# The shared expert's loads: a semaphore for each matrix, issued between the parts of the output weights

## The reference

```python
x = x + attn(layernorm(x), w_qkv, w_out, decay)     # linear attention with a decay
x = x + moe(layernorm(x), gate_w, w_gate, w_up, w_down, sw_gate, sw_up, sw_down)
# attn: q, k, v = x @ w_qkv; q, k = elu(q) + 1, elu(k) + 1
#       running_kv, running_k = scans over the tokens with decay sigmoid(decay) per head
#       out = (q * running_kv / clip(sum(q * running_k), 1e-6)) @ w_out
# moe:  8 experts of width 352, the best 2 of each token, weighed with their softmax scores
#       shared = (silu(x @ sw_gate) * (x @ sw_up)) @ sw_down, sw_gate and sw_up 512 x 704,
#       sw_down 704 x 512; out = routed + shared
```

## Time and profile before

| | |
|---|---|
| median of 3 runs | 714.49 us (713.29 to 715.1) |
| the profiled execution | 715.02 us, its span 713.2 us |
| mean granted TensorE clock | 0.972 |
| busy: PE, DVE, ACT, POOL | 663.0, 426.6, 257.1, 231.0 us |
| moved by DMA | 86.89 MB, 122 GB/s on the mean |

### The profile page before, as it was taken

One profiled execution on the slowest core, in us unless ns is written; L12 is line 12 of the kernel. 1 busy time (PEld: TensorE's weight loads), 2 busy tenths in 40 slices (PEclk: granted clock), 3 DMA queues, 4 the chain that ended last, 5 costly groups with the idle time before them and its releaser, 6 DMA issues.

```text
span 713.2 us, 11766 instructions
## 1 busy us (share of the span) xinstructions
PE 663.0 (93%) x3797; PEld 432.7 (61%) x3798; DVE 426.6 (60%) x746; ACT 257.1 (36%) x397; POOL 231.0 (32%) x269
## 2 busy tenths in 40 slices
PE   7868999899989989899999899999999999999992
PEld 6646677578657465556565465665656565656561
DVE  7757996997987753677787777633333333333331
ACT  5336263354342343546665665421111111111110
POOL 6201121322101313334343254124444444444431
PEclk9999999989989899999999999999999999999997
DMA  6561003513422497897564433268777777777753
GB/s 222 174 231 31 16 16 88 160 48 89 107 71 74 109 256 156 213 229 183 146 171 121 95 46 67 47 117 132 132 132 132 132 132 132 132 135 132 133 89 42
DMA packets 111236, 86.89 MB, mean 122 GB/s; under 512 B 79280, under 2 KB 86448, under 8 KB 111200
## 3 DMA queue, kind: packets, MB, share of 16 engines
q1 hardware_dynamic: 88848, 43.94, 25.7%
q0 software_dynamic: 12272, 27.34, 22.6%
q10 hardware_dynamic: 10080, 15.14, 6.8%
HBM read 44.45 MB, written 23.33 MB: 95 GB/s over the span
## 4 chain that ended last, share of the span: by engine, by line
PE 69%; DVE 8%; issue 2%; ACT 2%; DMA 1%; POOL 1%; ACTq 1%; SPq 0%; POOLq 0%; DVEq 0%
PE ps_y L514 17%; PE ps_g L514 16%; PE ps_u L514 15%; PE ring L389 14%; PE turn_h L534 3%; DVE routed L1409 1%; ACTq L373 1%; PE ps_norm L401 1%; DMA out_dram<-y_job,job_tok 1%; PE ps_den L450 1%; PE ring L476 0%; DMA xg_odd<-xn_hl 0%; DVE den L1304 0%; ACT xn L1040 0%; POOL squares L952 0%
## 5 line engine op out<-in xcount | busy, mean ns | idle before, releaser
L1349 DVE TENSOR_TENSOR hidT<-turn_h,hidT 128x384 f16<-128x384 f32 x71 | 39.5, 556 | 112.0 <-ACT hidT L1096 109.8
L945 POOL DMA_INDIRECT out_dram<-y_job,job_tok x39 | 61.9, 1586 | 109.1 <-DVE y_job L1683 102.2
L1092 ACT ACTIVATE silu<-ps_g,job_silu 128x352 f32<-128x352 f32 x39 | 21.6, 553 | 189.5 <-PE ps_g L514 158.9
L389 PE MATMUL ring<-xnT_h,wq_h 128*128 128x512 f32 x192 | 82.0, 427 | 7.5 <-DVE wq_l L1248 2.5
L514 PE MATMUL ps_y<-routed,hidT 128*128 x351 | 82.1, 379 | 1.3 <-DVE hidT L1349 1.3
L855 POOL TENSOR_SCALAR var_eps<-mean_var 128x1 f32<-128x1 f32 x32 | 12.9, 402 | 203.4 <-DVE mean_var L1339 114.9
L389 PE MATMUL ring<-xnT_l,wq_h 128*128 128x512 f32 x192 | 78.6, 410 | 0.0
L389 PE MATMUL ring<-xnT_h,wq_l 128*128 128x512 f32 x192 | 78.3, 408 | 0.0
L514 PE MATMUL ps_g<-routed,x_in 128*128 x468 | 76.4, 313 | 0.0
L514 PE MATMUL ps_u<-routed,x_in 128*128 x468 | 76.2, 313 | 0.0
L952 POOL TENSOR_TENSOR squares<-squares 128x704 bf16<-128x704 bf16 (+1 forms) x24 | 42.3, 1761 | 93.1 <-ACT squares L1060 93.1
(11 more groups left out here) (232 smaller groups left out, 1108.7 us busy)
## 6 DMA issues: line engine op xcount, KB each, us to landing
routed<-in_L_ffn_w_gate_dram ACTq DMA_DIRECT2D x7, 704.0 KB, 4.8
routed<-in_L_ffn_w_up_dram ACTq DMA_DIRECT2D x7, 704.0 KB, 7.7
x_res<-in_L_attn_x_dram SPq DMA_DIRECT2D x18, 256.0 KB, 3.2
out_dram<-x SPq DMA_DIRECT2D x16, 256.0 KB, 3.3
xn_scratch<-xn_hl SPq DMA_DIRECT2D x16, 256.0 KB, 2.4
out_dram<-y_job POOLq DMA_DIRECT2D x16, 256.0 KB, 4.2
x_in<-in_L_attn_x_dram SPq DMA_DIRECT2D x14, 256.0 KB, 2.7
routed<-in_L_ffn_w_down_dram ACTq DMA_DIRECT2D x7, 512.0 KB, 8.9
```

Of the source, the lines that this page charges most:

```text
L389: ins = pe.matmul(ps, a, b, start=(i == 0), stop=(i == len(steps) - 1))
L945: pool.indirect_dma_start(out[:, :], bass.IndirectOffsetOnAxis(job_tok[:, r:r + 1], 0), y_job[:, b, :], None, compute_op=ALU.add).then_inc ...
L1092: act.activation(silu[:, :], ps_g[:, 0:F], ACT.Silu, scale=by).then_inc(s["silu_s"], 1)
L1349: dve.tensor_tensor(hidT[:, 1], turn_h[:, 0:FC, :], hidT[:, 0], ALU.subtract).then_inc(s["hidT_s"], 1)
```

## The change

`shared_in` is replaced by `shared_g`, `shared_u` and `shared_d`, one for gate, up and down. Where SP before issued parts 13, 14, 15, waited for `over_0` and then issued the six shared loads, it now issues gate, part 13, up, part 14, waits for `over_0`, issues the four loads of down and then part 15. Before each square of the shared expert ACT waits for the semaphore of that piece's matrix, where before it waited for all six loads ahead of the first square.

```diff
-            gw_h_s ... cst_a cst_b shared_in
+            gw_h_s ... cst_a cst_b shared_g shared_u shared_d
...
-        SHARED_DMAS = 2 + 2 * HALVES
+        DOWN_DMAS = 2 * HALVES
...
             load_x(TPB)
             load_x(TPB + 1)
-            loads = [(shared[:, GAP + HALVES * at:GAP + HALVES * (at + GU)].rearrange("p (k f) -> p k f", f=HALVES * F),
-                      src.rearrange("(k p) f -> p k f", p=P)) for at, src in ((GATE_AT, sw_gate), (UP_AT, sw_up))]
+
+            def load_shared(at, src, done):
+                sp.dma_start(shared[:, GAP + HALVES * at:GAP + HALVES * (at + GU)]
+                             .rearrange("p (k f) -> p k f", f=HALVES * F),
+                             src.rearrange("(k p) f -> p k f", p=P)).then_inc(s[done], 16)
+
+            def load_shared_down(h):
+                for dst, src in down_parts(shared_raw[HALVES * 2 + h], sw_down[h * F:(h + 1) * F, :]):
+                    sp.dma_start(dst, src).then_inc(s["shared_d"], 16)
+
+
+            load_shared(GATE_AT, sw_gate, "shared_g")
+            load_part(QKV_PARTS + 1)
+            load_shared(UP_AT, sw_up, "shared_u")
+            load_part(QKV_PARTS + 2)
+            sp.wait_ge(s["over_0"], 1)
             for h in range(HALVES):
-                loads += down_parts(shared_raw[HALVES * 2 + h], sw_down[h * F:(h + 1) * F, :])
-            for m in range(QKV_PARTS + 1, PARTS):
-                load_part(m)
-            sp.wait_ge(s["over_0"], 1)
-            for dst, src in loads:
-                sp.dma_start(dst, src).then_inc(s["shared_in"], 16)
+                load_shared_down(h)
+            load_part(QKV_PARTS + 3)
...
                 x, kind, h, w, done = pieces[m]
+                if m < SHARED_PIECES:
+                    act.wait_ge(*((s["shared_g"], 16), (s["shared_u"], 16), (s["shared_d"], 16 * DOWN_DMAS))[kind])
                 if m == 0:
-                    act.wait_ge(s["shared_in"], 16 * SHARED_DMAS)
                     act.wait_ge(s["over_0"], 1)
```

More of the change, by code:

```diff
@@ L249, in preln_decay_attention_moe @@
             al_s out_mm xr0 xr1 x2_s stat2 var2 veps2 rstd2_s shift2_s norm2_s hi2_s xn2_s xg0 xg1 gw_sq_s gw_mm gw_set
-            gw_h_s gw_l_s gate_mm logit_s x2_out0 x2_out1 xn2_out0 xn2_out1 pad_out cst_a cst_b shared_in
+            gw_h_s gw_l_s gate_mm logit_s x2_out0 x2_out1 xn2_out0 xn2_out1 pad_out cst_a cst_b shared_g shared_u shared_d
             over_0 w0 w1 w2 w3 w4 w5 w6 w7 square_s fold_s norm_mm max_s set_s upper_s split_s
```

## The result

The changed kernel took 705.74 us (median of 4 executions, 701.55 to 709.1), the kernel before 714.16 beside it (713.29 to 715.1). The ratio is 0.9866 with a 95% interval of 0.9832 to 0.99: on the 714.49 us that the prediction started from that is 704.9 us, 9.6 us faster (7.1 to 12.0), where 7.3 were forecast. The direction was right and the gain was larger than the range allowed (its low end was 705.7).

The account below looks back on a forecast made before the run. TensorE, busy 93% of 713.2 us, bounds the kernel; only its idle time and slow clock can be won. 5.95 + 1.1 + 0.4 = 7.5 us off the 714.49 median gives 707.0; forecast 707.2, range 705.7 to 710.0.

Parts of the forecast that it names:

- low end: Fastest time of the range, 705.7 us: 8.5 us of gain from the median, less 0.3 for three runs' spread.
- The stall, its chain and its size: ScalarE's 9.2 us wait at the first shared square holds VectorE's fold and TensorE's column norms; removing it wins 7.5 us.
- the sum: Gain up to tile 6's transpose: 5.95 us TensorE idle, 1.1 slow clock, 0.4 VectorE work, together 7.5 us.
- What each half does: Split semaphores free ScalarE but not VectorE, which needs x tile 6 behind the fold; the earlier issue must pay for that.
- The queue: Shared loads on SP's queue fill the gap: gate lands at 29.4, or 31 with the landing; x tile 6 at 41.7.
- rival E: Gate and up delay the last Q part on the queue: 2.0 us slower, 716.5, up to 720; chance 0.04.
- D: Another load of the stream, tile 6 or part 13, replaces the last one: nothing gained, about 714 us; chance 0.03.
- rival C: x tile 6 becomes VectorE's new wait, landing at 44 to 46: gain only 3.5 to 5.5 us; chance 0.11.
- that edge: At `stats_x(6)` on VectorE, tile 6 costs nothing until 42.1 us, and one for one after that.
- rival B: Slow clock falls behind TensorE's wait before tile 6's transpose instead, costing 1.4 us: gain 6.1 us; chance 0.22.

Follow-up runs that it names:

- order alone: Changed kernel with its new issue order, but all six shared loads waited for ahead of the first square: 705.66 us, ratio 0.9886.
- tile 6 ahead: Changed kernel with part 15 and x tile 6 issued ahead of the four down loads: 707.48 us, ratio 0.9902.
- the filled stall: Kernel before with wide unread matmuls in TensorE's waits, 23 of them in the 5.95 us stall: 708.61 us, ratio 0.9944.
- The semaphores alone: Changed kernel with the shared loads issued where they were before, after parts 13, 14, 15: 711.33 us, ratio 0.9977.
- the fourteen: Profiles of the kernel before, the changed kernel and their variants, compared by slow time behind tile 6; their line is rest = 645.7 + 0.33 x slow.
- The three profiles of the changed kernel: Changed kernel without edit, run first and then twice more for more executions: medians 705.74, 704.14 and 706.4 us.
- wide fillings: Unread matmuls of 512 or 352 columns put into TensorE's waits: 708.61 us for the kernel before, 699.31 for the changed one.
- narrow fillings: Unread matmuls of 64 columns put into TensorE's waits: 710.38 us for the kernel before, 703.38 for the changed one.

## Why the prediction was right and wrong

**The stall, its chain and its size: right.** Two of the changed kernel's variants have the slow stretch where the kernel before had it, at 24 to 28 us, and full clock from there to tile 6 (order alone 52.43, tile 6 ahead 52.50; the prediction said 52.4). That is 7.5 us less than 59.97, and 7.5 was the sum. The terms have another meaning than I gave them. I counted TensorE's idle time, 1.1 us of slow clock and 0.4 of DVE; the filled stall shows that in the kernel before the slow clock there was covered by DVE. Before, the path was DVE's: its use of the relu moved from 55.55 to 48.05. DVE got rid of the stall of 8.18 and a wait of 0.31, now waits 0.66 us for the relu, and came to this stretch 0.45 us later (`lo_w(13)` at 40.50 for 40.05): 7.4, and 0.1 is the overlap of two instructions. The sum came out right because both roads end in the same relu.

**What each half does: right as far as it went.** The semaphores alone only move the wait to tile 6 (7.08 us), as said. The order alone has the whole gain, which the prediction did not ask: with the gap used, the last piece of down is there at 39.7 us, 1.3 after ACT wants gate, and the waits of the others cover that.

**The queue: right.** Gate was issued at 20.76 and took 8.1 us, so it lay there at 28.9 (said: 29.4, or 31 with the landing):

```profile
20.76 0.45 SPq L785 DMA_DIRECT2D shared<-in_L_ffn_sw_gate_dram  x1
shared<-in_L_ffn_sw_gate_dram SPq DMA_DIRECT2D x1, 1408.0 KB, 8.1
```

The last Q part landed where it had (ACT stood 5.50 us for it, 5.49 before), so rival E, and D, did not happen.

**Tile 6 (rival C): the place right, the price nothing.** It landed at 40.9 (said: 41.7), DVE stood 1.09 us, and moving it forward gave 0.1 or 0.2 us at most at the transpose. Beyond that edge the price there is one for one, as said.

**The clock (rival B): this step failed.** The prediction said that the clock's place "differs from one execution to the next", gave it one wait and one sign, a loss of 1.4 us, and a low end of 1 us below the sum, with 0.3 for the spread of three runs, for everything else. All other slow stretches it put at nothing. But the profile of before had 23.3 us of slow busy time behind tile 6, as much as any of the fourteen, and there was more to win there than to lose. The three profiles of the changed kernel had 10.0 to 15.8 us; at 0.33 us for each that is 2.5 to 4.4 us of gain. In the first of them the lead of 11.8 us is the 7.5 of the stall, 1.5 for the early slow stretch that a wait hid, and 2.9 behind tile 6, of which the 7.5 us less of slow time make 2.5. Neither of the last two was in the forecast. Rival B itself did happen in the profile of the changed kernel (0.52 from 50.60 to 57.40), and cost 2.7 us there, as two stretches and not one (1.4 was the price for one). With the spread that all executions show (2.9 us), the term should have been 0, give or take 4 us for a median of four; the range would then have begun at 703.

**What stays open.** The mean gain over all executions, 8.6 us (7.0 to 10.2), is compatible with 7.5, and a difference of a microsecond between them can't be settled by these. The two kernels with wide fillings differ by 9.3 us in their medians and 10.1 in their means, more than the 6.3 I expected from idle time alone (that figure fell with the terms above; 7.5 would have been right) and more than 7.5. I had written ahead of the run that 8 us or more would mean a part of the gain that is neither the stall nor the clock, and by that measure this pair speaks for such a part; the narrow fillings (7.0 in the medians) don't. In their profiles tile 6 is turned 58.84 - 52.45 = 6.4 us apart with, in the second alone, the unhidden slow stretch before 30 us, worth about 1.5 (52.5 against 51.0 in the table), so 7.9; the kernel before then has 3.4 slow microseconds more, and stands 2.0 us for the turning of a later tile by DMA:

```profile
PE ps_gate L503 <- DMA xg_odd<-xn_hl: 2.0, 1, 2.0
```

In the thirteen other profiles this wait is 0.2 or 0.3 us, in those of the kernel before and its narrow filling too, so it is no property of the old stall. Whether it comes with the wide fillings of that kernel in all its executions, or in this one alone, wasn't tried, and so the cause of its extra time and of its spread is open.

## What to carry to other kernels

When a late transfer is waited for by several, splitting its semaphore moves the wait to whoever stands behind the same queue; ask what lands last before and after, and put the bytes that are wanted late behind the ones wanted early. Where an idle queue has a gap in front of the stall (here 26.5 to 32 us), issuing into the gap is the gain. Before giving a gain of a per cent, look at how much slow clock the reference profile has: this kernel, which idles TensorE for 1 to 3 us in several places, ranged from 707.1 to 719.6 us, and a few wide matmuls in those waits took the changed kernel from 705.3 to 699.0 us on the mean, nearly as much as this change.

## What the hardware showed beside

Waits of 1.4 to 2.8 us were enough for a slow stretch of 3.4 us behind them, sometimes two in a row (6.8 us), and the same wait in the same kernel was followed by one in some executions and not in others: the wait of 1.42 us at 134.0 in the first profile of the changed kernel was, the one of 1.43 at 131.2 in the third was not. The six executions with tile 6 ahead all had a clock of 0.972 to 0.974, and five of six of the changed kernel beside them, with the same TensorE program, 0.981 to 0.983. Whether executions taken together agree by chance or the order of the loads does it isn't shown; either way four executions may say less than their spread suggests. Matmuls of 64 columns took 0.03 us each and kept the clock up badly (2.09 us of them in the stall, slow from 47.4 to 54.2); those of 512 columns did it (23 in 5.51 us, clock 1.00 from 41.8 to 48.3). Whether it is the width or the share of the wait that they fill wasn't tried:

```profile
41.80:48.30 6.50, 5.53 (x25) 4.24 (x23) 0.52 (x2) 1.93 (x3) 0.00 (x0) 1.00 0.53 153
```
